# Second attention: the product of the first rolled key with the queries moved from VectorE to ScalarE and GpSimd

## The reference

```python
def _L0_attn_b_ref(x, Wq, Wk, Wv, Wo, bo):      # x: 16 sequences x 256 tokens x 128
    N, S, D = x.shape
    H, hd = 16, D // 16                          # 16 heads of 8 features
    q, k, v = ((x @ W.T).reshape(N, S, H, hd).transpose(0, 2, 1, 3) for W in (Wq, Wk, Wv))
    att = jnp.einsum('nqhd,nkhd->nhqk', q, k)    # q, k: heads; h: tokens
    att = jax.nn.softmax(att / jnp.sqrt(hd), axis=3)
    out = jnp.einsum('nhqk,nkhd->nqhd', att, v).reshape(N, S, D)
    return out @ Wo.T + bo
```

## Time and profile before

| | |
|---|---|
| median of 3 runs | 973.76 us (971.58 to 976.4) |
| profiled execution | 972.47 us, span 970.7 us |
| granted TensorE clock, mean of the span | 0.929 |
| busy in the span | TensorE 799.1, VectorE 682.4, ScalarE 472.6, GpSimd 408.9 us |

### The profile page before, as it was taken

One profiled execution on the slowest core, in us unless ns is written; L12 is line 12 of the kernel. 1 busy time (PEld: TensorE's weight loads), 2 busy tenths in 40 slices (PEclk: granted clock), 3 DMA queues, 4 the chain that ended last, 5 costly groups with the idle time before them and its releaser, 6 DMA issues.

```text
span 970.7 us, 25469 instructions
## 1 busy us (share of the span) xinstructions
PE 799.1 (82%) x10228; PEld 614.3 (63%) x10228; DVE 682.4 (70%) x1560; ACT 472.6 (49%) x801; POOL 408.9 (42%) x302
## 2 busy tenths in 40 slices
PE   2899999999999999999995876668888888839655
PEld 1687777877788777877774453534555555525434
DVE  4677666676666766676664776548999999967763
ACT  1667666676666766776661423023333433315220
POOL 1445444444455444454442100018877778851000
PEclk9999999999999999999997977679999999957786
DMA  6000000000000000000000000000111111120002
GB/s 264 2 3 1 0 0 0 0 0 0 0 0 0 0 0 0 0 0 0 1 2 2 1 0 1 1 1 11 17 18 20 22 22 18 20 27 1 1 1 87
DMA packets 71586, 13.17 MB, mean 14 GB/s; under 512 B 66432, under 2 KB 70528, under 8 KB 70912
## 3 DMA queue, kind: packets, MB, share of 16 engines
q1 hardware_dynamic: 71552, 12.71, 6.0%
HBM read 8.51 MB, written 4.19 MB: 13 GB/s over the span
## 4 chain that ended last, share of the span: by engine, by line
PE 67%; DVE 19%; issue 6%; ACT 5%; POOL 3%; DMA 1%; DVEq 0%; SPq 0%; ACTq 0%; POOLq 0%
PE PS L525 6%; PE PS L482 6%; PE PS L341 6%; PE PS L342 5%; PE PS L343 5%; PE PS L418 4%; DVE b_prod L811 4%; PE PS L704 3%; PE PS L518 3%; PE PS L713 3%; PE PS L504 3%; PE PS L508 2%; PE PS L506 2%; PE PS L695 2%; PE PS L489 2%
## 5 line engine op out<-in xcount | busy, mean ns | idle before, releaser
L626 POOL TENSOR_TENSOR a_pl<-a_p,a_ph 128x1024 f16<-128x1024 f32 (+1 forms) x128 | 210.4, 1644 | 273.5 <-ACT a_ph L551 273.5
L858 POOL TENSOR_TENSOR b_w<-b_v,b_e 128x2048 f32<-128x2048 f32 x32 | 137.7, 4306 | 6.8 <-ACT b_e L773 6.8
L548 ACT ACTIVATE a_p<-PS 128x1024 f32<-128x1024 f32 (+1 forms) x128 | 103.8, 811 | 75.6 <-PE PS L489 75.5
L593 DVE TENSOR_REDUCE a_nm<-PS 128x4 bf16<-128x512 f32 (+1 forms) x128 | 121.3, 947 | 0.0
L541 ACT ACTIVATE a_qk_h<-PS 128x512 f16<-128x512 f32 x128 | 73.3, 604 | 79.5 <-PE PS L343 78.6
L551 ACT ACTIVATE a_ph<-PS 128x1024 f16<-128x1024 f32 (+1 forms) x128 | 103.0, 804 | 0.0
L811 DVE TENSOR_TENSOR b_prod<-PS,b_qt 128x512 f32<-128x512 f32 x128 | 83.0, 678 | 15.8 <-PE PS L697 15.0
L341 PE MATMUL PS<-xh,a_wqk_h 128*128 128x256 f16 x256 | 70.8, 277 | 27.1 <-DVE xl L577 26.9
L582 DVE TENSOR_TENSOR a_qk_l<-PS,a_qk_h 128x512 f16<-128x512 f32 x128 | 87.0, 681 | 2.8 <-ACT a_qk_h L541 2.8
L364 POOL TENSOR_TENSOR veps<-mv,eps 128x2 f32<-128x2 f32 (+2 forms) x40 | 7.9, 198 | 189.4 <-DVE mv L1132 137.1
L695 PE MATMUL PS<-b_kh,w_rolls 128*128 128x256 f16 x256 | 64.7, 281 | 20.6 <-DVE b_prod L811 19.7
(11 more groups left out here) (220 smaller groups left out, 2060.7 us busy)
## 6 DMA issues: line engine op xcount, KB each, us to landing
scratch_dram<-b_o SPq DMA_DIRECT2D x32, 64.0 KB, 3.5
b_y<-scratch_dram SPq DMA_DIRECT2D x16, 128.0 KB, 2.1
out_dram<-X SPq DMA_DIRECT2D x2, 1024.0 KB, 3.9
w_rest<-rest_dram SPq DMA_DIRECT2D x1, 1846.0 KB, 14.6
X<-x_dram SPq DMA_DIRECT2D x1, 1792.0 KB, 10.7
w_first<-first_dram SPq DMA_DIRECT2D x1, 1600.0 KB, 6.6
w_rolls<-rolls_dram SPq DMA_DIRECT2D x1, 512.0 KB, 15.2
X<-x_dram SPq DMA_DIRECT2D x1, 256.0 KB, 3.1
```

The lines of the kernel that those rows point to most:

```text
L548: act.activation((a_p0, a_p1)[j][:, me, :, :, :].rearrange("p a h q -> p a (h q)"), TT[:, :, 0:512 - 256 * j], ACT.Exp, scale=EA ** -0.5)
L593: dve.tensor_reduce(a_nm[:, nx, j, :].rearrange("p (a h) -> p a h", a=2)[:, :, 0:2], MM[:, :, 0:256 * (j + 1)].rearrange("p a (h k) -> p a ...
L626: pool.tensor_tensor(*(n[:, g % 2, :, :, :].rearrange("p a h q -> p (a h q)") for n in (pl, p, ph)), ALU.subtract).then_inc(a_split, 1)
L858: pool.tensor_tensor(b_w8[:, j, :, :, :], rolled_values(par, j, 0, H), rolled_exps(par, j, 0, H), ALU.mult).then_inc(b_weighed, 1)
```

## The change

ScalarE copies bank T[0] after `early` into a new SBUF buffer `b_kr`, and GpSimd multiplies that with the queries, in the step `early`, which on both engines stands before the rest of the trip. VectorE's roll 0 is gone. TensorE's instructions are the same, but roll 2 now waits for the copy (`b_copied`) where it waited for VectorE's product, and dots 0 waits for GpSimd too (`b_pooled`). `pe`, `act`, `dve` and `pool` in the diff are TensorE, ScalarE, VectorE and GpSimd.

```diff
+        b_kr = sb("b_kr", [128, 2 * SEQ])
...
                 elif kind == "early" or kind == "roll" and j > 0:
-                    m = ROLLS * (b + 1) + j
                     if j == 0:
                         pe.wait_ge(b_lo, b + 2)
-                    wait(pe, b_multiplied, m - 1)
+                    if j == 2:
+                        pe.wait_ge(b_copied, b + 2)
+                    else:
+                        wait(pe, b_multiplied, (ROLLS - 1) * (b + 1) + (j - 2 if j > 2 else j - 1))
...
                 elif kind == "dots":
-                    pe.wait_ge(b_multiplied, ROLLS * (b + 1) + 4 * j + 4)
+                    pe.wait_ge(b_multiplied, (ROLLS - 1) * (b + 1) + 4 * j + 3)
+                    if j == 0:
+                        pe.wait_ge(b_pooled, b + 2)
...
+                elif kind == "early":
+                    act.wait_ge(b_rolled, ROLLS * (b + 1) + 1)
+                    wait(act, b_pooled, b + 1)
+                    act.activation(b_kr[:, :], T[0][:, :], ACT.Copy).then_inc(b_copied, 1)
...
-                elif kind == "roll":                                    # VectorE
+                elif kind == "roll" and j > 0:
                     dve.wait_ge(b_rolled, ROLLS * (b + 1) + j + 1)
-                    if j == 0:
+                    if j == 1:
                         dve.wait_ge(b_q, b + 2)
-                    if j % 4 == 0:
+                    if j in (1, 4):
                         wait(dve, b_dotted, 2 * b + j // 4 + 1)
...
+                elif kind == "early":
+                    pool.wait_ge(b_copied, b + 2)
+                    wait(pool, b_dotted, 2 * b + 1)
+                    pool.tensor_tensor(b_prod[:, 0, :, :], b_kr[:, :].rearrange("p (e t) -> p e t", e=2),
+                                       b_qt[:, 1 - par, :].unsqueeze(1).to_broadcast([128, 2, SEQ]),
+                                       ALU.mult).then_inc(b_pooled, 1)
```

More of the change, by code:

```diff
@@ L633, in build @@
         b_stats, b_rstd, b_normed = sem("b_stats"), sem("b_rstd"), sem("b_normed")
-        b_q = sem("b_q")
+        b_q, b_copied, b_pooled = sem("b_q"), sem("b_copied"), sem("b_pooled")
         b_xh, b_xl, b_hi, b_lo, b_values = sem("b_xh"), sem("b_xl"), sem("b_hi"), sem("b_lo"), sem("b_values")
```

## The result

The changed kernel took 978.95 us as the median of 11 runs (976.24 to 981.55), against 973.51 for 11 runs of the kernel before beside it (970.91 to 976.4): a ratio of 1.006 [1.0047, 1.0073], 5.4 us slower. Measured again later, it was 979.74, ratio 1.0047 [1.003, 1.0064]. The forecast was 973.3, and 978.95 lies at the top end of its range; the gain of 0.5 us that was forecast against the kernel before was a loss. The ratio given with a run is against executions of the kernel before beside it, and can differ a little from the quotient of two medians in this text.

The account below looks back on a forecast made before the run. VectorE was fullest, but the transfer to `yt` would bind at 13.19 us against 13.28. Sequences 3 to 13 -1.0, sequence 14 +0.3 to +0.4, entry +0.15: sum -0.5, forecast 973.3 us, range 969 to 979.

Parts of the forecast that it names:

- What VectorE loses: VectorE without roll 0: 0.35 us a sequence gained, the rest becomes a wait; period 12.93 if nothing else binds.
- what ScalarE gains: ScalarE's PSUM copy, 597 ns, hidden under cover of over 2 us; its own cost nothing.
- The product: GpSimd's 128x512 multiplication, taken as 1.14 to 1.16 us from a subtraction's row; `weigh` 0 begins 1.26 later.
- The transfer's loop: GpSimd's output through SyncE's store and load to TensorE's `yt`, over two sequences: 26.38 us, 13.19 each against 13.28.
- Alternating short and long: Sign at `soft`: every 13.2 us on average, perhaps in turn, since a late `soft` gives the transfer more time.
- the wait of about 1 us at `yt`: Sign on TensorE: it waits about 1 us for the DMA of `b_y` in most sequences.
- Before sequence 3 the loop has no transfer yet: Stage entry: GpSimd's `b_w` up to 1.3 us later, values of sequences 1 and 2 wait; +0.15, 0.5 either side.
- GpSimd's loop: Values, copy, product, norm, both `weigh` and back to the values: 12.94 to 12.96 us, costing nothing by itself.
- rival (c): TensorE's clock falls through the longer `yt` wait in each sequence: +12 us, thus 985; chance 0.06.
- Tail: Sequence 14: no norm and no gain there, but its `yt` is late all the same; +0.3 to +0.4 us.
- (a): The transfer doesn't hold TensorE, so GpSimd's loop decides: -3.9 us, 969.9; chance 0.14.
- (b): GpSimd's product costs more, setting the period from 1.62 us on; at 2.1, +8 us, thus 982; chance 0.09.

Follow-up runs that it names:

- gpsimd_pad: The kernel before with an idle 128x512 multiplication on GpSimd between the norm and `weigh` 0; 975.54 us, ratio 1.0019.
- yt_later: The changed kernel with TensorE's steps `yt`, `apply` and `project` moved behind roll 3; 975.49 us, ratio 1.001.
- busy_wait: The changed kernel with 24 idle TensorE matmuls ahead of the third interval's late `yt`, the loop's first turn written out; 979.07 us, one execution.
- before_again: The kernel before, unchanged, profiled a second time; 973.44 us.
- after_5: The changed kernel, unchanged, run once more later, timed and profiled; 979.74 us, ratio 1.0047.
- entry_by_vector: The changed kernel, but VectorE makes the first product from PSUM as before for the rolled keys of sequences 0, 1 and 2; 978.88 us, ratio 1.0057.
- entry_tail_by_vector: As entry_by_vector, with VectorE also making the first product in the rolls during sequence 14; 979.77 us, ratio 1.0057.
- both_yt_later: entry_tail_by_vector with TensorE's `yt`, `apply` and `project` moved behind roll 3; 973.47 us, ratio 1.0007.
- entry_busy: entry_by_vector with 20 idle TensorE matmuls ahead of the wait at sequence 3, the loop's first turn written out; 978.18 us, one execution.
- vector_product: The changed kernel, but VectorE multiplies ScalarE's copy from SBUF as roll 0 and GpSimd gets nothing; 979.52 us, ratio 1.0062.

## Why the prediction was wrong, by its own steps

**What VectorE loses, what ScalarE gains: right.** Roll 1 waited 0.33 and gather 1 came at 751.47 - 749.16 = 2.31 after `soft`, against 2.25 worked out. The copy took 0.605, and TensorE's and VectorE's rolls did not wait for it in the steady part.

**The product: mis-sized, 1.27 for 1.14 to 1.16.** The subtraction of the earlier trace rows was the nearest row, not the same form. The same size without the broadcast operand took 1.04 (gpsimd_pad). The ratio in the Trainium skill ("GPSIMD Engine Reference", Elementwise), 1.96 at 2048 elements, gave 1.33 as an estimate in the prediction; the row here, 1270 against 679 ns, is 1.87 times, closer to the page than to the row I chose.

**The transfer's loop: right in kind, 0.12 a sequence short.** GpSimd around 750:

```profile
750.81 1.27 POOL L863 TENSOR_TENSOR b_prod<-b_kr,b_qt 128x512 f32<-128x512 f32 x1 [1.82 <-ACT b_kr L776]
...
753.38 4.31 POOL L873 TENSOR_TENSOR b_w<-b_v,b_e 128x2048 f32<-128x2048 f32 x1
757.65 0.62 POOL L856 TENSOR_TENSOR b_o<-b_s,b_rs 128x256 f32<-128x256 f32 x1
```

SyncE's store of one output and the load behind it:

```profile
744.76 1.30 SPq L1240 DMA_DIRECT2D scratch_dram<-b_o  x2
749.22 0.36 SPq L1245 DMA_DIRECT2D b_y<-scratch_dram  x1
```

TensorE's weight load that waits for it, as in the earlier trace rows:

```profile
751.35 0.20 PEld L727 LDWEIGHTS PS<-w_first,b_y 128*128 128x128 f32 x2 [0.90 <-DMA b_y<-scratch_dram]
```

The load issued at 749.22 is 749.22 - 735.47 = 13.75 after the `soft` of its sequence and is used 2.13 later, at 15.88 where I had 15.57; of that difference 0.12 is the product. Two sequences take 13.69 + 13.00 = 26.69 here where I had 26.38. Alternating short and long (in the first half of the stage), the wait of about 1 us at `yt` and the clock of 1.00 came as written. Eleven intervals thus gave +0.3 (146.38 against 146.09; +0.1 as the mean of three executions each) instead of -1.0: a term mis-sized by 1.1 to 1.3 us. That it is the transfer which takes most of what VectorE gives is shown by yt_later, where the period is 13.07.

**The step that failed: "Before sequence 3 the loop has no transfer yet, ... I count +0.15, with 0.5 to either side."** The third interval was 16.5 to 17.7 where the kernel before has 13.32, and there most of the loss lies. GpSimd there, in order of time:

```profile
659.49 8.57 POOL L873 TENSOR_TENSOR b_w<-b_v,b_e 128x2048 f32<-128x2048 f32 x2
669.37 1.27 POOL L863 TENSOR_TENSOR b_prod<-b_kr,b_qt 128x512 f32<-128x512 f32 x1 [1.32 <-ACT b_kr L776]
...
671.95 4.31 POOL L873 TENSOR_TENSOR b_w<-b_v,b_e 128x2048 f32<-128x2048 f32 x1
```

ScalarE's values, SyncE's load and TensorE's `yt`:

```profile
668.15 0.66 ACT L770 ACTIVATE b_v<-PS 128x256 f32<-128x256 f32 x2 [1.28 <-POOL b_w L873]
...
681.14 0.66 ACT L770 ACTIVATE b_v<-PS 128x256 f32<-128x256 f32 x2 [1.58 <-POOL b_w L873]
```
```profile
681.38 0.36 SPq L1245 DMA_DIRECT2D b_y<-scratch_dram  x1
```
```profile
683.58 0.61 PE L727 MATMUL PS<-w_first,b_y 128*128 128x128 f32 x2 [2.77 <-DMA b_y<-scratch_dram]
```

GpSimd of the kernel before at the same place, its `soft` being at 664.48:

```profile
656.16 8.57 POOL L858 TENSOR_TENSOR b_w<-b_v,b_e 128x2048 f32<-128x2048 f32 x2
...
667.28 4.30 POOL L858 TENSOR_TENSOR b_w<-b_v,b_e 128x2048 f32<-128x2048 f32 x1
```

and its values:

```profile
664.82 0.66 ACT L765 ACTIVATE b_v<-PS 128x256 f32<-128x256 f32 x2
```

The first interval is 11.33, 1.6 shorter than the 12.95 of GpSimd's loop, so that its `b_w` pair ends at 659.49 + 8.57 = 668.06, past the `soft` at 666.37; before, it ended at 664.73 and the values went on at once. `v` waits for it (I had named that wait), and everything that I had put in one row behind `v` follows: copy, product, norm, `weigh` 0. It began 671.95 - 666.37 = 5.58 after `soft`; in the profile before it was 667.28 - 664.48 = 2.80. The output is late by 2.8, not by 1.26, since the wait for the values and the product add up. The load was issued at 681.38, 2.15 after the next `soft`, and TensorE had it at 683.58, 4.35 after it; it stood 2.77 us with roll 2, `project` and roll 3 behind it. I had counted that delay only for the values, and not followed it to the first transfer, that of sequence 0, which TensorE wants in this very interval; that "the loop has no transfer yet" there was wrong. Behind the wait the clock fell to 0.50 and 0.72, which busy_wait prices at about 1.4 of the 3.3 us. That part of rival (c) I had given 0.06 and looked for in every sequence; it struck once. Both parts were at hand before the result: the first interval of 11.10 stood in the trace, and so did the 12.95 of the new loop.

The step had also a bad base: I took the fall to 0.79 in the kernel before for a feature of it, and it was one execution's; before_again had 1.00 there and 13.11 for the interval.

**Tail: +0.8 where I had +0.3 to +0.4**, by gpsimd_pad the effect of a later `weigh` alone.

The sum by its own terms: steady +0.3, second interval -0.25, third +3.3, last +0.8, first +0.1: +4.3 against before_again, and the stages differ by 200.86 - 196.60 = 4.26. The medians differ by 5.4 and 6.0. The rest, about 1 us, is not explained. By the three profiles each it lies behind the last `soft`: 122.7 us on average against 120.5, and ahead of the first `soft` nothing (653.7 against 654.1). In that last part the changed kernel had the lower clock: from 60 to 80 us behind the last `soft` 0.75, 0.74 and 0.74, where the kernel before had 0.91, 0.83 and 0.91. Why, no run shows. And after_5 shows that a late clock fall in the last interval adds 2 us in some executions.

Of the rivals, (a) fell (the transfer does hold TensorE), and (b) fell as priced: the product stood at 1.27, not above 1.62. Open is how much of the loss at the first late transfer would come back if the entry were served otherwise: in entry_by_vector, entry_tail_by_vector, both_yt_later and entry_busy it came back one interval on, but in each of them that transfer also took 0.9 to 1.1 us longer from store to load (5.33 to 5.53), and no run has the one without the other. No version that computes the whole product was faster than the kernel before; the nearest are both_yt_later and yt_later with 1.0007 and 1.001.

## What to carry to other kernels

A loop that just fits when it is closed can still cost much where it starts: work out the first two or three trips one by one, with the waits that add up in them, and carry the delay to the first transfer that depends on it. Before work goes from the fullest engine to another, ask whether a transfer waits for that other engine, and what stands behind the reader of the transfer; here the fullest engine's 0.35 us a sequence was paid for by 1.27 on the way to the store, and with the reader moved behind two more rolls 0.2 a sequence was kept in the middle of the stage. And before a lone odd interval is built on, look at it in a second execution.

## What the runs showed of the hardware

GpSimd's time for a product of f32 with 128 rows differed by the operands as well as by the size: 0.322 us for 64 columns and 1.27 for 512 with one operand broadcast, 1.04 for 512 of one buffer multiplied by itself, 4.31 for 2048. Which property of the operands makes the 0.23 was not separated. The norm's `rstd` on GpSimd took 0.70 us in most kernels and 1.02 beside VectorE's product with both inputs in SBUF (vector_product; 1051 ns as the mean of 11). The Trainium skill, "SBUF — State Buffer", Practical consequences, says that a VectorE instruction with two SBUF inputs contends with a GpSimd instruction that reads SBUF, and one with at most one SBUF input outside the 2-port modes does not. The traces agree: beside products with an input in PSUM `rstd` stayed at 0.696 us in both kernels, and `b_w` at 4.31.

From SyncE's store to its load it is 4.47 us in nearly all sequences. In seven of the kernels above one such pair took longer, 5.07 to 5.75; in six of them it was the second of the stage, the one that the fourth interval waits for. In entry_by_vector it was 693.39 - 688.02 = 5.37:

```profile
688.02 1.34 SPq L1252 DMA_DIRECT2D scratch_dram<-b_o  x2
693.39 0.36 SPq L1257 DMA_DIRECT2D b_y<-scratch_dram  x1
```

Instruction packets moved then too (70 GB/s from 690 to 691, where a store alone, that of the kernel before from 701 to 703, has 54), so a fetch of code beside the store is the likely cause, argued from the times and not tested by itself.
